# A perceiver block: GpSimd folds each head's summed probabilities to 512 columns, and the order of the maximum tiles on TensorE moves by one

## The reference

```
x = x + cross_attention(layernorm(x), context)   # 16 heads of width 32, 256 queries, 4096 keys
x = x + causal_attention(layernorm(x))           # 16 heads of width 128 in 4 groups
x = x + swiglu(layernorm(x))                     # inner width 2048
# one head of the cross attention, all in fp32:
p = exp(q @ k.T / sqrt(32) - maximum of the row)
o = (p @ v) / (sum of p over the 4096 keys)
```

## Time and profile before

| | |
|---|---|
| median of 3 runs | 602.35 us (602.3 to 602.77) |
| the profiled execution | 602.53 us, span 600.5 us |
| busy in the span (the page) | TensorE 98%, VectorE 64%, ScalarE 50%, GpSimd 44% |
| mean granted TensorE clock | 1.000 |
| from 191.8 to 402.0 us (210.2 us) | TensorE 208.85 us busy, VectorE 186.54, GpSimd 173.92, ScalarE 128.62 |

### The profile page before, as it was taken

The page is one execution under the profiler, slowest core; times in us unless marked ns, Lnnn a source line. Parts: engine busy times, 40 slices in busy tenths (PEclk is TensorE's granted clock), DMA queues, the critical chain, the costliest instruction groups (busy, mean ns, idle before and its releaser), DMA issues.

```text
span 600.5 us, 12582 instructions
## 1 busy us (share of the span) xinstructions
PE 585.7 (98%) x4269; PEld 469.8 (78%) x4270; DVE 384.6 (64%) x688; ACT 301.7 (50%) x439; POOL 266.9 (44%) x142
## 2 busy tenths in 40 slices
PE   8999999999999999999999999999999999999997
PEld 7888888888887667666776676766898889799996
DVE  4999430340434888888888888897664235475562
ACT  3544233233233566556666655565368677645441
POOL 0000933113124888788888888870103644400000
PEclk9999999999999999999999999999999999999999
DMA  8865734524638654545554555500142224245410
GB/s 289 328 229 189 221 126 168 198 95 166 191 125 270 201 166 153 180 156 169 160 153 153 158 169 161 155 38 1 35 176 72 86 106 160 83 199 211 159 50 36
DMA packets 34223, 92.20 MB, mean 154 GB/s; under 512 B 6928, under 2 KB 11024, under 8 KB 30480
## 3 DMA queue, kind: packets, MB, share of 16 engines
q1 hardware_dynamic: 32944, 89.68, 45.2%
q10 hardware_dynamic: 1248, 2.10, 0.9%
HBM read 65.02 MB, written 18.35 MB: 139 GB/s over the span
## 4 chain that ended last, share of the span: by engine, by line
PE 86%; ACT 4%; DVE 4%; issue 2%; POOL 2%; DMA 1%; ACTq 0%; POOLq 0%; SPq 0%; DVEq 0%
PE ps L348 16%; PE ps L349 15%; PE ps L350 15%; PE ps L1578 10%; PE ps L1566 10%; PE ps L1440 9%; PE ps L1592 3%; ACT p_ring L785 3%; POOL l_ring L680 2%; PE ps L1544 1%; DVE m_part L1067 1%; PE ps L1649 1%; DMA f_ring<-stream 1%; PE ps L1458 1%; PE ps L1532 1%
## 5 line engine op out<-in xcount | busy, mean ns | idle before, releaser
L1067 DVE TENSOR_REDUCE m_part<-ps 128x1 f32<-128x512 f32 x240 | 150.8, 683 | 20.5 <-PE ps L1440 20.2
L785 ACT ACTIVATE p_ring<-ps 128x1024 f32<-128x1024 f32 x128 | 124.5, 1022 | 69.2 <-PE ps L1578 28.7
L634 POOL TENSOR_TENSOR p_sum<-p_sum,p_ring 128x1024 f32<-128x1024 f32 x42 | 100.1, 2383 | 3.7
L1566 PEld LDWEIGHTS ps<-q_stack,k_stack 98*128 98x128 f32 x512 | 75.0, 189 | 16.3 <-ACT p_ring L785 6.6
L1566 PE MATMUL ps<-q_stack,k_stack 98*128 98x256 f32 x512 | 85.2, 289 | 1.3
L1440 PE MATMUL ps<-k_stack,q_max 96*128 96x512 f32 x240 | 85.5, 417 | 0.1
L609 POOL TENSOR_TENSOR v_all<-v_all,bv_row 128x512 f32 (+1 forms) x32 | 41.7, 1320 | 74.8 <-ACT v_all L747 74.3
L1578 PE MATMUL ps<-p_ring,v_head 128*32 128x256 f32 x960 | 64.6, 383 | 0.0
L1026 DVE SCALAR_TENSOR_TENSOR kl_buf<-ps,biases,kh_buf 128x512 fp32r<-128x512 f32 x32 | 23.7, 749 | 56.0 <-ACT kh_buf L735 55.6
L348 PE MATMUL ps<-xt_h,h_ring 128*128 128x256 f32 x200 | 57.0, 285 | 1.8 <-POOL l_ring L680 1.8
L321 DVE TENSOR_TENSOR l_ring<-f_ring,h_ring 128x2048 fp32r<-128x2048 f32 x22 | 50.2, 2288 | 12.5 <-ACT h_ring L317 12.5
(11 more groups left out here) (225 smaller groups left out, 1168.1 us busy)
## 6 DMA issues: line engine op xcount, KB each, us to landing
f_ring<-stream SPq DMA_DIRECT2D x29, 1024.0 KB, 4.9
k_stack<-kh_scratch SPq DMA_DIRECT2D x128, 128.0 KB, 2.6
kh_scratch<-kh_buf SPq DMA_DIRECT2D x32, 256.0 KB, 5.7
kl_scratch<-kl_buf SPq DMA_DIRECT2D x32, 256.0 KB, 6.1
k_stack<-kl_scratch SPq DMA_DIRECT2D x64, 128.0 KB, 2.6
v_head<-v_all SPq DMA_DIRECT2D x16, 512.0 KB, 2.9
v_all<-stream SPq DMA_DIRECT2D x4, 256.0 KB, 4.7
f_ring<-stream SPq DMA_DIRECT2D x4, 256.0 KB, 5.8
```

What stands on the lines that cost most here:

```text
L634: nc.gpsimd.tensor_tensor(p_sum[:, p, :], p_ring[:, 0, :] if n == 0 else p_sum[:, p, :], p_pair[:] if c == 3 else p_ring[:, c % 4, :], ALU ...
L785: nc.scalar.activation(p_ring[:, c % 4, :], ps[:, 2 * (c % 2):2 * (c % 2) + 2, :].rearrange("p b n -> p (b n)"), ACT.Exp, scale=XSCALE).th ...
L1067: nc.vector.reduce_max(m_part[:, j // NT, j % NT:j % NT + 1], maximum_bank(j), AX.X).then_inc(max_read, 1)
L1566: last = nc.tensor.matmul(ps[:, 2 * (c % 2) + k // 2, (k % 2) * N:(k % 2 + 1) * N], k_stack[p][0:SPLIT_ROWS + MAX_ROWS, at128(4 * c + k)], ...
```

## The change

GpSimd does a sixth operation for each head but the last: it adds columns 512 to 1023 of the head's sum onto columns 0 to 511. The four ones-products on the sum then take 128 columns each, two for each half of the queries. At the end of a head TensorE makes tiles 0 to 4 of the head after next instead of 0 to 3; tile 2 stands between values 6 and the maximum rows, tiles 3 and 4 stand behind value 7. The tiles of the next head move by one accordingly, and so does VectorE's order.

```
-NSUMS = len(SUM_CHUNKS) - 1
-SUMS_BEFORE = (-2, -1, 0, None, 1, 1, None, None)
+NSUMS = len(SUM_CHUNKS)
+SUMS_BEFORE = (-3, -2, -1, None, 1, 1, None, None)
...
+            def fold_sum(h, p, adds):
+                pool.wait_ge(sums_done, NSUMS * h + adds)
+                nc.gpsimd.tensor_tensor(p_sum[:, p, 0:2 * N], p_sum[:, p, 0:2 * N], p_sum[:, p, 2 * N:4 * N],
+                                        ALU.add).then_inc(sums_done, NSUMS - adds)
...
             def summed_denominators(h, p):
                 pe.wait_ge(sums_done, NSUMS * h + NSUMS)
-                denominators(p_sum[:, p, :]).then_inc(sums_used, 1)
+                for k in range(4):
+                    half = k % 2
+                    last = nc.tensor.matmul(bank(7)[k * DH:(k + 1) * DH, N + half * P:N + (half + 1) * P], ones_col[:],
+                                            p_sum[:, p, k * P:(k + 1) * P], start=False, stop=False,
+                                            skip_group_check=True)
+                last.then_inc(sums_used, 1)
...
                 score(3)
-                next_maxima(9, 10)
+                next_maxima(10, 11)
                 if not first:
                     summed_denominators(h - 1, 1 - p)
-                next_maxima(10, 12)
+                next_maxima(11, 12)
                 score(4)
-                next_maxima(12, 13)
+                next_maxima(12, 14)
                 score(5)
-                next_maxima(13, 15)
+                next_maxima(14, 15)
...
                 for c in range(4, 7):
                     value(c)
+                maxima_after(2, 3)
                 maximum_rows(h + 1)
                 value(7)
-                if after_loads is not None:
-                    maxima(h + 2, p, after_loads, 2, 4)
+                maxima_after(3, 5)
```

More of the change, by code:

```diff
@@ L636, in sum_chunks @@
                                             ALU.add).then_inc(sums_done, 1)
+                fold_sum(h, p, NSUMS - 1)
+            def fold_sum(h, p, adds):
+                pool.wait_ge(sums_done, NSUMS * h + adds)
+                nc.gpsimd.tensor_tensor(p_sum[:, p, 0:2 * N], p_sum[:, p, 0:2 * N], p_sum[:, p, 2 * N:4 * N],
+                                        ALU.add).then_inc(sums_done, NSUMS - adds)
             def sum_chunks_in_two_pairs(h, p):
@@ L651, in sum_chunks_in_two_pairs @@
                 nc.gpsimd.tensor_tensor(p_sum[:, p, :], p_sum[:, p, :], p_pair[:],
-                                        ALU.add).then_inc(sums_done, NSUMS - 3)
+                                        ALU.add).then_inc(sums_done, 1)
+                fold_sum(h, p, 4)
             for g in range(KT):
@@ L1128, in _ @@
             negate_maximum(0)
-            chunk_maxima(1, 0, 4)
+            chunk_maxima(1, 0, 5)
             def add_pair(h):
@@ L1145, in head @@
                 first = isinstance(h, int) and h == 0
-                chunk_maxima(h + 1, 4, 12)
+                chunk_maxima(h + 1, 5, 12)
                 add_pair(h)
@@ L1156, in head @@
                 if after:
-                    chunk_maxima(h + 2, 1, 4)
+                    chunk_maxima(h + 2, 1, 5)
             head(0)
@@ L1608, in value, with maxima_after @@
                     values(h, p, loads, c)
+                def maxima_after(start, end):
+                    if after_loads is not None:
+                        maxima(h + 2, p, after_loads, start, end)
                 score(0)
-                next_maxima(4, 5)
+                next_maxima(5, 6)
                 score(1)
-                next_maxima(5, 7)
+                next_maxima(6, 8)
                 score(2)
-                next_maxima(7, 9)
+                next_maxima(8, 10)
                 score(3)
-                next_maxima(9, 10)
+                next_maxima(10, 11)
                 if not first:
                     summed_denominators(h - 1, 1 - p)
-                next_maxima(10, 12)
+                next_maxima(11, 12)
                 score(4)
-                next_maxima(12, 13)
+                next_maxima(12, 14)
                 score(5)
-                next_maxima(13, 15)
+                next_maxima(14, 15)
                 for c in range(4):
@@ L1627, in head @@
                 next_maxima(15, 16)
-                if after_loads is not None:
-                    maxima(h + 2, p, after_loads, 0, 1)
+                maxima_after(0, 1)
                 score(6)
@@ L1633, in head @@
                 score(7)
-                if after_loads is not None:
-                    maxima(h + 2, p, after_loads, 1, 2)
+                maxima_after(1, 2)
                 for c in range(4, 7):
                     value(c)
+                maxima_after(2, 3)
                 maximum_rows(h + 1)
                 value(7)
-                if after_loads is not None:
-                    maxima(h + 2, p, after_loads, 2, 4)
+                maxima_after(3, 5)
             def last_values(p, loads, c):
@@ L1696, in _ @@
             pe.wait_ge(ones_set, 3)
-            maxima(1, 1, 1, 2, 4)
+            maxima(1, 1, 1, 2, 5)
             head(0, 0, 1, 1, 2, first=True)
```

## The result

The changed kernel takes 613.19 us (median of 4 runs, 612.07 to 616.66) against 602.38 (602.3 to 602.77, 4 runs): a ratio of 1.0188, 95% interval 1.0156 to 1.022, so it is slower by 1.9%. The forecast was 611.2 us with a range of 603.5 to 614.5.

What follows compares the result with a forecast made beforehand. TensorE's own program order bound the head at 14.11 us; with the change a VectorE-GpSimd ring of 14.65 us would. Pair ends +1.1 us in head 1, +7.9 by head 14, +8.8 in all: 611.2 us, range 603.5 to 614.5.

Steps and rivals of the forecast that it cites:

- The ring: VectorE and GpSimd wait on each other: pair end to last addition 9.88, fold 1.32, first addition 2.37, pair 1.08: 14.65 us.
- Two-input exclusion: VectorE's pair add, reading two SBUF tiles, and GpSimd's addition exclude each other; the pair ends 1.08 us behind GpSimd's.
- TensorE alone: TensorE's own time per head: 14.11 + 0.34 - 0.21 = 14.24 us, +1.6 us over the kernel.
- Exit and entry: Switching from 32-column values to tile 2 and back on TensorE: 0.34 us in heads 0 to 13, +4.8 us.
- the rest is order only: On TensorE, tiles 3 and 4 replace 2 and 3 ahead of a head's first scores; the first exponential's wait stays.
- The saving of 3.2 us on the products: Summed products on TensorE with half the columns: 0.21 us saved in each of 15 heads, bounds 0 and 0.21.
- The wait at tile 2: TensorE's moved tile 2 waits some 0.3 us for the normalized outputs, bringing TensorE's head to 14.55 us.
- The sum: Pair ends later by 1.1 us in head 1 and 7.9 by head 14; with the last head +8.8 us.
- Stalls: TensorE waits for the fold at the summed products: 0.9 us in the first head, 1.1 us in the last.
- TensorE the bound: Rival: pair and first addition hardly delay each other, heads 14.24 us; 606.6 us, or 609.8 in a third; chance 0.17.
- The fold late by 0.6 us a head: Rival: pair no earlier relative to S (start of a head's first scores), TensorE stalls, heads 14.84 us; 614 us; chance 0.10.
- Faster: Rival: VectorE's reads one tile further on remove 0.41 us idle weight loads ahead of tiles 10 and 15; 598 us; chance 0.12.

Runs made afterwards that it cites:

- experiment 4: Kernel before plus GpSimd's extra addition, written to an unused buffer with nobody waiting, products still 256 columns: 610.96 us, ratio 1.0142.
- experiment 2: Kernel before with the tile order of the change, without the fold and with products of 256 columns: 606.97 us, ratio 1.0078.
- experiment 1: Fold only: the changed kernel (fold and products of 128 columns) with the tile order of before: 612.88 us, ratio 1.017 against before.
- experiment 5: Kernel before plus the unread GpSimd addition, with VectorE's pair add written as a one-input reduction: 616.03 us, ratio 1.0223 against before.
- experiment 8: Kernel before with the change's tile order, no fold, but tiles 2, 3 and 4 all behind value 7: 606.05 us, ratio 1.0053.
- experiment 3: Kernel before with products of 128 columns and no fold, leaving columns 512 to 1023 of the sum out: 600.65 us, ratio 0.9973.
- experiment 6: Changed kernel, but head 14's sum isn't folded and the last head takes it with 256-column products: 611.01 us, ratio 1.0146 against before.
- experiments 7: Kernel before with score group 0 moved ahead of maximum tile 3 instead of behind it: 602.87 us, ratio 1.0003.

## Why the prediction was right, and where its sizes were off

The ring was the cause. GpSimd's addition alone, with no reader, gives the same 14.72 us a head as the whole change (experiment 4), and the new order alone gives 14.44 (experiment 2). The fold without the new order gives 14.72 too (experiment 1), but there TensorE's wait for the fold would by itself give nearly as much, so it adds little to the proof. Two-input exclusion is part of it: the pair adds end 1.07 to 1.09 us behind GpSimd's addition in all three, and don't collide when they are a reduction (experiment 5).

That the forecast of 611.2 us is within 2 us of the median is right by its mechanism; at full clock it is 0.9 us off. But the clock, which the prediction didn't have, adds about 1 us to the median, and the longest of the four runs, 616.66 us, lies above the range of 603.5 to 614.5. Had a second of the four been like it, the median would have lain above the range; that none was is luck.

- **TensorE alone, 14.24 us a head.** At 14.72 TensorE waits about 0.2 us for the fold and 0.2 for the output, which leaves 14.3. Exit and entry measured 0.33 to the forecast 0.34, but with 0.06 of waiting in it, and the products 0.35 us to the forecast 0.36. By the Trainium skill ("TensorE: Matmul & The Clock Gate", The mechanism) loads overlap matmuls only across row groups. The trace does not bear that out: 0.35 against 0.57 us shows that the loads of 108 ns stay hidden under half the streaming. But "the rest is order only" was wrong in itself: the extra tile costs 0.25 by bank waits when it isn't split off (experiment 8). The sum was right since the split replaces that cost, which the prediction did not know: here it was lucky.
- **The saving of 3.2 us on the products** was mis-sized as a gain of the kernel: alone it gives 1.7 (experiment 3), probably since VectorE's reads follow closely. In the sum it didn't matter, as the ring sets the head.
- **The wait at tile 2.** The prediction's own terms give 12.05 - 11.89 = 0.16 us between the outputs and TensorE; it wrote "some 0.3" and so 14.55 us for TensorE's head instead of 14.40. The measured 0.2 us fits its terms. The ring sets the head either way, so the sum didn't suffer.
- **The ring, 14.65 us.** Forecast 9.88 + 1.32 + 2.37 + 1.08; in the same cut, from the pair's end, 10.00 + 1.24 + 2.39 + 1.09 = 14.72. 0.07 us off, over 13 heads 0.9 us.
- **The sum.** Head 1's pair ends at 214.60 (forecast 214.36), head 14's at 405.99 (404.81), and the summed products of the last head start at 415.96 against 405.78, +10.2 us; at full clock it ends as +9.7 us against the forecast +8.8.
- **Stalls.** Head 1: 0.6 for 0.9 us, since TensorE got there at 210.6 instead of 210.1: in head 0 two pairs of tiles took 0.72 us to the next start (196.53 to 197.25, 197.73 to 198.45) instead of 0.47, like those of experiment 8. Last head: 1.10 us, as forecast. Not foreseen was that the clock falls behind this stall in some executions, for up to 4.6 us; without it (experiment 6) the time is 611.01 us.
- **What would show it.** Pair adds were 1.87 us for "about 1.7"; pair ends 14.72 apart for 14.6 to 14.7. "GpSimd without idle time ahead of the pair, but for some 0.2 us" contradicts the prediction's own terms: a tail of 1.08 us plus the semaphore is 1.25, and the trace shows 1.25.
- **Rivals.** TensorE the bound: no, heads are 0.4 us longer than it alone needs. The fold late by 0.6 us a head: it is late by 0.2, and the pair does come earlier relative to S, at 315.82 - 310.32 = 5.50 for the forecast 5.46. Faster: no; the idle loads ahead of tile 15 stayed at 0.41 us. Ahead of tile 11 they are down to 0.20, but so they are behind the halved products of experiment 3, where the trace names no semaphore; together they are 7.3 us in 24 times instead of 9.9. As TensorE's reordering in experiments 7 and 8 shows, the real bank waits come on top of them.

The Trainium skill ("GPSIMD Engine Reference", Key points) names the shared SBUF interfaces and, on VectorE's side, instructions with two SBUF inputs as those that contend. The traces agree: 1.87 against 1.22 us for the addition with two inputs, and 2.33 to 2.34 beside GpSimd and alone for the reduction with one.

No kernel here beats before; experiment 3 is shorter, but leaves out half of the sum.

## What to carry to other kernels

Idle time of an engine is free only if nothing that runs there now overlaps an operation that it excludes, and if the idle time isn't the tail of a wait that closes a ring: follow one period around (producer, helper, back), add durations and tails, and compare with the bottleneck's own period before spending it. When several limits lie within 0.1 to 0.3 us of each other, as TensorE's order, VectorE's reads and GpSimd's ring do here, removing one wait gives half or nothing, and an edit must be measured alone as well as together. And a stall of about 1 us of a TensorE that is otherwise never idle may cost more than its length.

## What the runs showed of the hardware

- TensorE's granted clock fell from 1.00 to 0.50 (2.4 to 1.2 GHz) right after a stall of 1.10 us in the last head in the profiled execution, and stayed there for some 10 us, with TensorE busy 2.00 of 2 us, at 4.5 us of cost. Behind the 1.07 us of fold only it fell too, for some 3.4 us. With the stall gone the mean clock was 1.000 in five of five runs. In which executions the clock falls stays open: two of the changed kernel's four runs and two of fold only's five kept 0.999 or 1.000, and a stall of much the same length does nothing in the trace of before: its TensorE waits 0.92 and 0.34 us ahead of 426.93 and 427.92, is busy 1.08 of 2 us from 425 to 427, and the clock stays at 1.00. What makes the difference no run shows.
- A two-input fp32 addition of 128x1024 on VectorE that starts while GpSimd adds ends 1.07 to 1.09 us behind GpSimd's end, whether it came 0.2, 0.8, 0.95 or 1.9 us ahead of that end (1.29, 1.88, 2.02 and, for the second pair of head 14 in the changed kernel, 2.97 us long): it hardly advances until GpSimd is through. A one-input reduction over the same data isn't held up, 2.33 us beside GpSimd and alone.
- Eight records of 128 columns over four column groups of 32 follow each other in 0.35 us, those of 256 in 0.57.
